# A decoder layer in one kernel: the experts' first layer over 64 rows, stores on SyncE, first inputs loaded ahead

## What is computed

```
x = x + xattn(ctx, layernorm(x))     # q, k, v, o projections 512 -> 512, softmax over keys j <= i
n = layernorm(x)
s = sigmoid(n @ W_enc + b_enc)                          # 512 -> 1024
c = s @ W_s2c + b_s2c                                   # 1024 -> 64
gate = top 2 of softmax(c @ Wr + br), normalised        # 8 experts
h_e = relu(c @ W1[e] + b1[e])                           # 64 -> 512, for every expert e
m = sum over e of gate_e * (h_e @ W2[e] + b2[e])        # 512 -> 64
d = sigmoid(m @ W_c2s + b_c2s) @ W_dec + b_dec          # 64 -> 1024 -> 512
x = x + layernorm(d, ln_g, ln_b)
```

## Time and profile before

| | us |
|---|---|
| median of 3 runs (3199.2 to 3202.05) | 3200.46 |
| the profiled execution | 3196.54 |
| its span, first to last instruction | 3194.9 |
| TensorE busy | 2996.2 (94%) |
| VectorE busy | 1813.1 (57%) |
| ScalarE busy | 1518.6 (48%) |
| GpSimd busy | 1620.7 (51%) |

### The profile page before, as it was taken

One profiled execution on the slowest core, in us unless ns is written; L12 is line 12 of the kernel. 1 busy time (PEld: TensorE's weight loads), 2 busy tenths in 40 slices (PEclk: granted clock), 3 DMA queues, 4 the chain that ended last, 5 costly groups with the idle time before them and its releaser, 6 DMA issues. The chain is left out here.

```text
span 3194.9 us, 42271 instructions
## 1 busy us (share of the span) xinstructions
PE 2996.2 (94%) x15688; PEld 1722.8 (54%) x15688; DVE 1813.1 (57%) x3439; ACT 1518.6 (48%) x2861; POOL 1620.7 (51%) x699
## 2 busy tenths in 40 slices
PE   7977999999999999999999999996858999999996
PEld 6865555554455554555544555532644666555653
DVE  3365888875687774788755788701642333233333
ACT  2232355666555666556666556663224333433332
POOL 1011167779567799467787577797531110111110
PEclk9988799999999999999999999997978999999998
DMA  4559234458544559344568344454983110111000
GB/s 184 201 182 269 77 101 115 113 121 177 142 116 105 122 120 208 108 116 101 122 146 170 110 118 98 112 117 122 321 270 89 53 53 1 53 54 53 27 27 14
DMA packets 133283, 384.04 MB, mean 120 GB/s; under 512 B 12224, under 2 KB 28096, under 8 KB 111584
## 3 DMA queue, kind: packets, MB, share of 16 engines
q0 software_dynamic: 36192, 222.05, 26.9%
q1 hardware_dynamic: 90048, 148.07, 17.0%
q10 hardware_dynamic: 6848, 11.31, 1.2%
HBM read 124.03 MB, written 79.17 MB: 64 GB/s over the span
## 5 line engine op out<-in xcount | busy, mean ns | idle before, releaser
L859 ACT ACTIVATE pT<-s_bank 128x512 f32<-128x512 f32 (+5 forms) x2176 | 1088.7, 581 | 722.7 <-PE s_bank L1019 548.0
L878 DVE TENSOR_REDUCE row_max<-m_bank 128x1 f32<-128x512 f32 (+4 forms) x2240 | 1258.5, 626 | 296.0 <-PE m_bank L972 166.0
L797 POOL TENSOR_TENSOR part_sum<-part_sum,pT 128x2048 f32<-128x2048 f32 x236 | 1103.3, 4675 | 119.4 <-ACT pT L859 112.0
L1019 PE MATMUL s_bank<-q_sb,k_sb 104*128 104x512 f32 (+3 forms) x2176 | 864.9, 426 | 18.6 <-ACT pT L859 15.8
L972 PE MATMUL m_bank<-k_sb,q_sb 96*128 96x512 f32 (+4 forms) x2240 | 811.9, 408 | 26.1 <-DMA q_sb<-qT_hi 20.8
L1019 PEld LDWEIGHTS s_bank<-q_sb,k_sb 104*128 104x128 f32 x2176 | 412.8, 192 | 295.9 <-ACT pT L859 205.6
L972 PEld LDWEIGHTS m_bank<-k_sb,q_sb 96*128 96x128 f32 x2240 | 423.7, 196 | 209.5 <-DVE row_max L878 118.9
L1036 PE MATMUL o_bank<-pT,v_sb 128*32 128x512 f32 (+5 forms) x4352 | 503.4, 580 | 0.0
L1421 POOL TENSOR_TENSOR f_var_eps<-f_mean_var,eps 128x4 f32<-128x4 f32 x8 | 1.6, 203 | 583.9 <-DVE f_mean_var L1585 583.9
L797 POOL TENSOR_TENSOR part_sum<-pT 128x2048 f32<-128x2048 f32 x28 | 127.8, 4564 | 266.9 <-ACT pT L859 216.7
L1036 PEld LDWEIGHTS o_bank<-pT,v_sb 128*32 128x32 f32 (+1 forms) x4352 | 114.0, 110 | 231.7 <-issue 146.5
(11 more groups left out here) (196 smaller groups left out, 3371.0 us busy)
## 6 DMA issues: line engine op xcount, KB each, us to landing
moved_sum<-pT POOLq DMA_DIRECT2D x168, 1024.0 KB, 7.0
q_sb<-qT_hi SPq DMA_DIRECT2D x64, 256.0 KB, 5.0
k_sb<-kT_hi SPq DMA_DIRECT2D x48, 256.0 KB, 8.6
qT_hi<-q_hi POOLq DMA_DIRECT2D x8, 1024.0 KB, 6.9
qT_lo<-q_lo POOLq DMA_DIRECT2D x8, 1024.0 KB, 9.0
q_sb<-qT_lo SPq DMA_DIRECT2D x32, 256.0 KB, 4.6
aT<-o_sb ACTq DMA_DIRECT2D x32, 256.0 KB, 5.1
a_in<-aT SPq DMA_DIRECT2D x8, 1024.0 KB, 9.2
```

The source lines that it names most:

```text
L797: pool.tensor_tensor(total, pT[:, slot(S - 1), :, q0:] if j and kt == 1 else total, pT[:, slot(S), :, q0:], ALU.add).then_inc(pool_added, 1)
L859: act.activation(pT[0:rows, slot(S), item, q0:], s_bank[(HG * S + item) % S_RING][0:rows, q0:], ACT.Exp, scale=SCALE).then_inc(exp_done, 1)
L878: dve.tensor_reduce(row_max[:, j % 2, r, h, c:c + 1], m_bank[p % M_BANKS][:, 0:n], AX_X, ALU.max).then_inc(unit_max, 1)
L1019: mm = pe.matmul(out[:, q0:], k_sb[0:R_END, h, at:at + P], q_sb[j % QBUFS][0:R_END, h, q0:], start=True, stop=kt < 4 * j)
```

## The change

- The stores of keys, values and queries are issued by SyncE, in the loops in which it loads context and x blocks, and no more by GpSimd. Because those stores may still run when the next stage starts, ScalarE and VectorE wait for the keys' and values' at the start of the query stage (keys_stored), and GpSimd for the queries' in the attention.
- The buffers of x, its normalised form (x_in, xn), of a_in, o_x_in, and of the encoder's input (f_x_hi, f_x_lo) are allocated by the caller; x_in and xn, and later a_in and o_x_in, lie in the place of the four query buffers q_sb. The first x block is loaded into x_in; its statistics and normalisation stand at the end of the key and value stage.
- The first query block is loaded in iteration 7 of the query stage, the first two blocks of the attention's result and the first x of the output stage in the last steps of the attention, the encoder's first input near the end of the output stage.
- W1 is loaded once, with the even experts on partitions 0 to 63 and the odd ones on 64 to 127, hi and lo parts in tensors of their own. A step of the first layer is six matmuls over 64 rows: three products, each for both halves in turn, into two banks.

```diff
-                def load_next(b, u, before, more):
+                def body(b, u, before, more):
                     if more:

                         hold(sp, c_lo_ready, DC * b, passed)
@@ -129,24 +129,22 @@
                             "(c p) n -> p c n", p=P)).then_inc(c_loaded[1 - u], 16)
                     else:
                         load_ahead(sp)
-                blocks(sp, load_next)
+                    n = BLK if more else N_LAST
+                    cols = bass.ds(b * BLK, n)
+
+                    hold(sp, bank_free, 4 + JOBS * b + DC, passed)
+                    sp.dma_start(kT_hi[:, cols].rearrange("(c p) n -> p c n", p=P), as_f32(k_hi[:, u, :, 0:n])).then_inc(k_stored[u], 16)
+                    sp.dma_start(kT_lo[:, cols].rearrange("(c p) n -> p c n", p=P), as_f32(k_lo[:, u, :, 0:n])).then_inc(k_stored[u], 16)
+
+                    hold(sp, bank_free, 4 + JOBS * b + DC + n // P, passed)
+                    sp.dma_start(v_dram[cols, :].rearrange("(t p) n -> p t n", p=P), v_out[:, u, 0:n // P]).then_inc(v_stored[u], 16)
+                blocks(sp, body)

             @block.gpsimd
             def _(pool):
                 pool.dma_start(bk_col[:, :], bk).then_inc(bias_loaded, 16)
                 pool.dma_start(bv_all[:, :], bv.partition_broadcast(P)).then_inc(bias_loaded, 16)
-
-                def store(b, u, before, more):
-                    n = BLK if more else N_LAST
-                    cols = bass.ds(b * BLK, n)
-
-                    pool.wait_ge(bank_free, 4 + JOBS * b + DC)
-                    pool.dma_start(kT_hi[:, cols].rearrange("(c p) n -> p c n", p=P), as_f32(k_hi[:, u, :, 0:n])).then_inc(k_stored[u], 16)
-                    pool.dma_start(kT_lo[:, cols].rearrange("(c p) n -> p c n", p=P), as_f32(k_lo[:, u, :, 0:n])).then_inc(k_stored[u], 16)
-
-                    pool.wait_ge(bank_free, 4 + JOBS * b + DC + n // P)
-                    pool.dma_start(v_dram[cols, :].rearrange("(t p) n -> p t n", p=P), v_out[:, u, 0:n // P]).then_inc(v_stored[u], 16)
-                blocks(pool, store)
+                rows.invert(pool, 0, 0)
...
+                rows.statistics(dve, 0, 0, 0)
+                rows.normalise(dve, 0, 0)
...
+    def statistics(self, dve, b, u, before):
+        dve.wait_ge(self.x_loaded[u], 16 * (before + 1))
+        for k in range(4):
+            dve.bn_stats(self.stats[:, u, k], self.x_in[u][:, k]).then_inc(self.stats_ready, 1)
+        hold(dve, self.stats_ready, 4 * (b + 1), self.passed_dve)
+        for k in range(4):
+            dve.bn_aggr(self.mean_var[:, u, k], self.stats[:, u, k]).then_inc(self.mv_ready, 1)
+
+    def invert(self, pool, b, u):
+        pool.wait_ge(self.mv_ready, 4 * (b + 1))
+        pool.tensor_tensor(self.var_eps[:, u], self.mean_var[:, u, :, 1], self.eps[:, :], ALU.add).then_inc(self.eps_ready, 1)
+        pool.wait_ge(self.eps_ready, b + 1)
+        pool.tensor_tensor(self.rstd[:, u], self.var_eps[:, u], self.neg_half[:, 0:4], ALU.pow).then_inc(self.rstd_ready, 1)
+
+    def normalise(self, dve, b, u):
+        dve.wait_ge(self.rstd_ready, b + 1)
+        for k in range(4):
+            dve.tensor_scalar(self.xn[u][:, k], self.x_in[u][:, k], self.mean_var[:, u, k, 0:1], self.rstd[:, u, k:k + 1],
+                              ALU.subtract, ALU.mult).then_inc(self.xn_ready, 1)
...

                         hold(sp, xn_ready, 4 * b, passed)
-                        sp.dma_start(x_in[:, 1 - u], x[bass.ds((b + 1) * BLK, BLK), :].rearrange(
+                        sp.dma_start(x_in[1 - u][:, :, :], x[bass.ds((b + 1) * BLK, BLK), :].rearrange(
                             "(t p) n -> p t n", p=P)).then_inc(x_loaded[1 - u], 16)
                     if isinstance(b, int) and b == 2 * PAIRS:

                         load_first(sp)
+                    if isinstance(b, int) and b == 2 * PAIRS + 1:
+                        load_first_block(sp)
+                    cols = bass.ds(b * BLK, BLK)
+
+                    hold(sp, q_lo_ready, 4 + DC * (b + 1), passed)
+                    sp.dma_start(qT_hi[:, cols].rearrange("(c p) n -> p c n", p=P), as_f32(q_hi[:, u])).then_inc(q_stored[u], 16)
+                    sp.dma_start(qT_lo[:, cols].rearrange("(c p) n -> p c n", p=P), as_f32(q_lo[:, u])).then_inc(q_stored[u], 16)
...
-                    cols = bass.ds(b * BLK, BLK)
-
-                    pool.wait_ge(q_lo_ready, 4 + DC * (b + 1))
-                    pool.dma_start(qT_hi[:, cols].rearrange("(c p) n -> p c n", p=P), as_f32(q_hi[:, u])).then_inc(q_stored[u], 16)
-                    pool.dma_start(qT_lo[:, cols].rearrange("(c p) n -> p c n", p=P), as_f32(q_lo[:, u])).then_inc(q_stored[u], 16)
...
+                for sem, n in keys_stored:
+                    act.wait_ge(sem, n)
...
-                for j in range(QBUFS):
+                for j in range(1, QBUFS):
...
+                    if g == NG - 1 and s == FIRST_STEP[QB - 1] + STORE + DEN_AFTER + 2:
+
+                        load_behind(sp)
...
+                for u in range(2):
+                    pool.wait_ge(q_stored[u], 32 * (QB // 2))
...
+                        hold(sp, a_lo_ready, DC * QB, passed)
+                        hold(sp, t_stored, 32 * (QB - 2), passed)
+                        load_behind(sp)
...
-                for n, stage in enumerate((y, hT)):
-                    for top in (0, M):
-                        act.dma_start(stage[top:top + M, :, :], w["W1"][n * E // 2:(n + 1) * E // 2].rearrange("e m n -> m e n")
-                                      ).then_inc(w1_loaded[n], 16)
+                w1 = w["W1"].rearrange("(p k) m n -> k m p n", k=2)
+                for k in range(2):
+                    act.dma_start(hT[k * M:(k + 1) * M, :, :], w1[k]).then_inc(w1_loaded, 16)
...
-                for n, stage in enumerate((y, hT)):
-                    act.wait_ge(w1_loaded[n], 32)
-                    act.activation(w1_parts[:, n * E // 2:(n + 1) * E // 2, :], stage[:, :, :], ACT.Copy).then_inc(w1_hi_ready, 1)
-
-                act.wait_ge(w1_lo_ready, 2)
+                act.wait_ge(w1_loaded, 32)
+                act.activation(w1_hi, hT[:, :, :], ACT.Copy).then_inc(w1_hi_ready, 1)
+
+                act.wait_ge(w1_lo_ready, 1)
...
+                dve.wait_ge(w1_hi_ready, 1)
+                dve.tensor_tensor(w1_lo, hT[:, :, :], as_f32(w1_hi), ALU.subtract).then_inc(w1_lo_ready, 1)
...
-                    def hidden(k):
-
-                        p, c, half = k // (2 * EC), k % (2 * EC) // 2, k % 2
-                        dst = bank(("w1", k))
-                        if k == 0:
-                            pe.wait_ge(w1_lo_ready, 2)
+                    def hidden(q):
+
+                        p, c = q // EC, q % EC
+                        dst = [bank(("w1", 2 * q + k)) for k in range(2)]
+                        if q == 0:
+                            pe.wait_ge(w1_lo_ready, 1)
                             pe.wait_ge(c_lo_ready, b + 1)
-                        for part in range(2):
-                            mm = pe.matmul(dst[:, :], w1_parts[:, 2 * p + half, c * P:(c + 1) * P], c_parts[:, part],
-                                           start=part == 0, stop=part == 1)
-                        mm.then_inc(ring_done, 1)
+                        for n, (ww, part) in enumerate(((w1_hi, 0), (w1_hi, 1), (w1_lo, 0))):
+                            for k in range(2):
+                                rows = slice(k * M, (k + 1) * M)
+                                mm = pe.matmul(dst[k][:, :], ww[rows, p, c * P:(c + 1) * P], c_parts[rows, part], start=n == 0, stop=n == 2)
+                                if n == 2:
+                                    mm.then_inc(ring_done, 1)
...
+        def load_output_inputs(sp):
+
+            for u in range(2):
+                hold(sp, a_stored[u], 16 * (QB // 2 * (NG - 1) + 3), inputs_passed)
+                sp.dma_start(a_in[u][:, :, :], aT[:, u * BLK:(u + 1) * BLK].rearrange("(c p) n -> p c n", p=P)).then_inc(a_loaded[u], 16)
+            sp.dma_start(o_x_in[0][:, :, :], a["x"][0:BLK, :].rearrange("(t p) n -> p t n", p=P)).then_inc(o_x_loaded[0], 16)
...
+            def load_first_block(sp):
+
+                hold(sp, rows.xn_ready, 4 * (QB - 1), passed)
+                hold(sp, q_stored[0], 32, passed)
+                load_query_rows(sp, 0, 0)
```

167 lines of the change are left out of this document (78 added, 89 removed).

## The result

| | before | after |
|---|---|---|
| median of 4 runs each, us | 3199.8 (3198.1 to 3202.1) | 3251.5 (3247.8 to 3261.6) |
| ratio to before, 95% interval | 1 | 1.0166 (1.0142 to 1.0190) |
| the profiled execution, us | 3196.5 | 3250.5 |
| its span; mean granted clock | 3194.9; 0.963 | 3248.9; 0.955 |

The account below looks back on a forecast made before the run. TensorE was taken as the bound, busy 94% of the span, standing still mostly at stage seams. Terms 4.4 + 77.5 - 11 - 3.5 + 3 - 9 - 27 = +34, added to the 3200.5 us median: 3235 us (8 in 10: 3198 to 3270).

Parts of the forecast that it names:

- Query stage, +77.5: Query stage: x loads wait behind each block's end and stores; six periods 12.9 us longer, +77.5 us (+39 to +90).
- T + 10.8: Query stage: the next x block lands 10.8 us after T, the end of a block's last low part.
- Rival 3: Query stage: x load doesn't queue behind the stores, lands by T + 6.8, clock stays up; 3194 us, chance 0.11.
- T + 6.8: Query stage: lower end for the x load's landing, 6.8 us after the end of a block's last low part.
- estimate of 9.2 us: Query stage: three 1 MB transfers in a row by the skill's fit, giving 3226 instead of 3235 us.
- First x block, +4.4: Query stage's start: 1.9 us later, and block 1's transposes at the low clock, +2.5; sum +4.4 us (0 to +7).
- Query to attention, -11: Seam into attention: no wait for GpSimd's last stores, first query block loaded early; -11 us (-5 to -17).
- Attention to output, and output to feed-forward: Two seams: early inputs -3.5 us; last output stores behind two x loads +3; 3 MB less to load in feed-forward -9.
- The experts' layer, -27: Experts' first layer: paired row halves run side by side, 0.23 us less in each of 128 steps; -27 us in sum.
- 3.9 from the 77%: Experts' first layer: six 64-row matmuls take 3.9 matmul times instead of 3; the layer saves 3 us.
- forecast as 2.4: Expert loop: ScalarE's two activations come 0.3 us later at the end of a block; +2.4 us.
- the 6 to 14 that were to show the forecast right: Attention's start: an idle time of 6 to 14 us was named as a sign of the forecast.

Follow-up runs that it names:

- e4_query_stores_only: Kernel before the change with one edit: SyncE issues the queries' two stores a block; 3274.1 us, ratio 1.0252.
- e1_query_stores_gpsimd: Changed kernel with one part undone: GpSimd issues the queries' stores again; 3169.2 us, ratio 0.9919.
- e2_x_load_before_stores: Changed kernel with SyncE's order turned: x block b + 2 is loaded before the wait for block b and its two stores; 3182.8 us, ratio 0.9960.
- e5_weights_after_spread: e1_query_stores_gpsimd with the loads of the second head group's first keys and of wo issued after the maximum row's first spread; 3171.5 us, ratio 0.9914.
- e6_keys_one_chunk_a_block: e2_x_load_before_stores with the 28 loads of first keys and values split, four behind each x load of blocks 0 to 6; 3174.0 us, ratio 0.9920.
- e3_experts_rows_only: Kernel before the change with only the experts' first layer over 64 rows, including W1's load and split; 3171.7 us, ratio 0.9925.

## Why the prediction was right, and where it was not

1. **Query stage, +77.5: right, measured +76.0.** The mechanism is that of the text: the load stands behind the wait for the block's end. The load is there 10.7 us after the end of the low parts (T + 10.8 was the estimate from the output stage), the clock falls, the transposes take 3.67 us. e4_query_stores_only shows the cause alone, e1_query_stores_gpsimd and e2_x_load_before_stores each take it away in another way. Rival 3 is out: x landed at T + 10.7, not T + 6.8, and a pause of 5.96 us ahead of block 1's transposes already had the lower clock behind it. From the first store's issue (231.61) to VectorE's start (242.22) it is 10.6 us. The prediction's estimate of 9.2 us for the three transfers came from the fit of the Trainium skill, "DMA: Bandwidth & Descriptors", section on the anatomy of one DMA, which is stated for a GpSimd DMA; for these three of SyncE the trace's 10.6 us does not agree with it.
2. **First x block, +4.4: right, +3.8.** The stage starts 2.3 us later and block 1's transposes run at the low clock.
3. **Query to attention, -11: wrong, +1.5.** The step that failed was the rate. The text let the queue carry 12.75 MB at 300 GB/s and land the first query block 43 us after the end of block 5. That end is 333.71; the last of the block's three loads landed at 386.42, 52.7 us later, which is 242 GB/s by the same count. So the idle time was 16.2 us, not 9: -3.8 instead of -11. Part of the 300 was a misreading: it divides what had been issued, not what had landed. In MB of 2^20 bytes 300 is 315 GB/s; the windows of the two traces (the last three columns are granted clock, DMA share and GB/s) give 288 over before's 28 loads and 259 over this stretch:

```profile
248.70:291.50 42.80, 41.52 (x203) 33.90 (x201) 26.42 (x50) 15.39 (x26) 7.06 (x10) 1.00 1.07 288
```

```profile
333.90:386.60 52.70, 24.36 (x105) 20.03 (x103) 13.24 (x24) 7.90 (x12) 1.77 (x5) 0.75 1.06 259
```

   At 288 GB/s the 12.75 MB take 46 us; why the rate fell further is not shown. There was a slip besides: by the prediction's own periods 43 us after the end of block 5 is 6 us behind the end of block 7, not 8. It hid 2 us of the miss.

   The other 5.3 us were no term of the sum at all: the first row maximum is not the end of the step. Behind it the maximum row is spread by a DMA on the same queue, behind the query rows, the next group's keys and wo, which SyncE had issued late. From the one to the other it is 23.3 us instead of 18.0. The last row is the first row maximum, and the argument ended there too. e5_weights_after_spread shows the queue's part, e6_keys_one_chunk_a_block that of the 28 loads.
4. **Attention to output, and output to feed-forward: right.** -2.5 by the end of the output stage's work, +3.8 for its stores behind the two loads, -10.6 to the first spikes (the terms were -3.5, +3 and -9). e3_experts_rows_only adds that some 7 of the last come from W1's halved load alone.
5. **The experts' layer, -27: right in kind, too large.** The step is the 1.90 us that was forecast: it is shorter by one matmul time, so six matmuls of 64 rows take three. The prediction had also worked out 3.9 from the 77% in the Trainium skill, "TensorE: Matmul & The Clock Gate", section on the measured speedup of packed matmuls; for these two row groups the trace's 0.89 us for six does not agree with it. Added up by group from the first hidden step to the end, after against before, hidden steps and router are 30.1 us less, where 29.5 were forecast. What was mis-sized is what the loop gives back, forecast as 2.4:
   - output steps +4.8, of which the wait for raw at the block's end is 3.0;
   - encoder and gate groups +4.8. The gates' chain through GpSimd and VectorE is now met by a shorter loop (waits +2.0 here, +4.2 in e3_experts_rows_only), and the encoder's matmuls follow each other at a slower pace (0.2333 us against 0.2305 before, some 2 us);
   - groups ahead of the first step behind the gates +3.8: a hidden step takes two banks of the ring at once and waits for the second (3.5).

   The ground for taking 3 was weaker than it reads. The four column-half matmuls of L1672 do overlap in the records, but by the earlier trace rows the next group starts 1.01 us behind them, 0.25 us each, no less than full-width ones one after the other take (0.230). They showed no gain that could be carried over to the rows. That the near value held is in part luck.

So the 19.6 us between sum and spans are 12.5 from the seam and 9.9 from the layer, less 2.8 from the rest. The two misses do not cancel each other; both make the kernel slower than forecast, and the 3251.5 us stand at the upper edge of the forecast's own range of 3212 to 3252. The idle time of 16.2 us at the attention's start is outside the 6 to 14 that were to show the forecast right.

## What to carry to other kernels

A store that waits for the end of a block must not stand, on the engine that issues it, ahead of a load that the next block needs; ask of every moved DMA which wait it is now queued behind, and issue the load first. A seam ends at the last thing that passes the queue, not at the first: follow it to the instruction that starts the next stage's bottleneck, take a queue's rate from what has landed and not from what has been issued, and keep large transfers that nobody needs yet behind the small one that somebody waits for. Where a loop gets shorter, list all the chains beside it that stay as long as they were.

## What was not expected of the hardware

Matmuls of one shape did not follow each other at one pace in all kernels. Over the query stage the mean distance of two matmuls of 128x512 was 0.2334 us in the kernel before and e3_experts_rows_only, and 0.227 in e1_query_stores_gpsimd, e2_x_load_before_stores and e6_keys_one_chunk_a_block; that is the 12.96 and 12.65 us of their periods. Rows of before, and under them of e1_query_stores_gpsimd, ten matmuls apart (2.33 and 2.26 us):

```profile
287.02 0.39 PE L416 MATMUL q_bank<-xT_hi,wq_lo 128*128 128x512 f32 x1
...
289.35 0.40 PE L416 MATMUL q_bank<-xT_hi,wq_hi 128*128 128x512 f32 x1
```

```profile
287.00 0.39 PE L428 MATMUL q_bank<-xT_hi,wq_lo 128*128 128x512 f32 x1
...
289.26 0.39 PE L428 MATMUL q_bank<-xT_hi,wq_hi 128*128 128x512 f32 x1
```

The window from 230 to 270 us of each (us; busy time of TensorE, its weight loads, VectorE, ScalarE, GpSimd; granted clock; DMA share; GB/s) shows the same clock, 1.00, and 4 matmuls and transposes more in the second:

```profile
230.00:270.00 40.00, 40.00 (x198) 33.04 (x198) 30.68 (x62) 14.14 (x24) 9.20 (x14) 1.00 0.92 278
```

```profile
230.00:270.00 40.00, 40.00 (x202) 33.83 (x201) 30.25 (x62) 14.81 (x25) 8.27 (x12) 1.00 0.85 266
```

In the feed-forward stage it is the other way round: the encoder's matmuls were 0.2295 us apart in e3_experts_rows_only and 0.2333 in the changed kernel, some 3 us over eight blocks; before they were 0.2305 apart. In both stages the instructions are the same and the tiles lie elsewhere in on-chip memory. That the place is the cause was not tried.
